# Before the first FFN: turning back by transposes, theta in the last head, the second bias behind both scales

## The chip, the cores and the metric

The kernel runs on one core of one Trainium2 chip. The metric is the device time in microseconds of one execution; several executions give a median. The profile is taken from one execution by the hardware profiler, and its times count from that execution's first instruction.

## What is computed

A block of four residual steps on x, 8 batches of 256 rows of 512 (2048 rows in all), with a context of the same shape:

```python
x = x + tanh(g_xattn[0]) * L0_xattn(ctx, ctx, layernorm(x), ssm_kernel, D, 8)
x = x + tanh(g_ffn[0])   * L0_ffn(layernorm(x), w1, b1, w2, b2)
x = x + tanh(g_xattn[1]) * L1_xattn(layernorm(x), ctx, theta, phi, g, ...)
x = x + tanh(g_ffn[1])   * L1_ffn(x, w1, g1, w2, g2, w3, g3)
```

The first step is a long convolution for each of 32 heads. The second quantises the normalised x by ONE scale for the whole tensor (max of all absolute values over 127), multiplies by int8 weights w1 (2048x512), adds b1, applies GELU, quantises by one scale again and multiplies by w2 (512x2048), with b2 added. `theta` is a product of the context alone: theta_w (128x256) by each batch's context, plus theta_b; step three uses it.

## The kernel before

The program is written by hand for each engine, with semaphores between them. The x residual stands in SBUF as 16 tiles of 128x512 (`x_res`); `order1` lists the first half of every batch's rows and then the second, so tiles n = 0 to 7 and n = 8 to 15 belong to one half each. Groups of four tiles share one computation of scales (`G` = 4, `NG` = 4).

**Heads.** TensorE computes 32 heads by 20 fp32 matmuls each (`head`, L1221 to L1237), VectorE multiplies (L1662), GpSimd and VectorE add halves into `qT`, and ScalarE repeats operands (L824, L846). Heads 20 to 27 carry the turning back of tiles 0 to 7 in spare PSUM columns (L1235), added to x by VectorE with a reversed reading of PSUM (`back_add`, L1702). ScalarE's loop over the heads (L897) also turns weights of the last FFN into ternary values (`ternary`, L885). SP's queue loads and stores those weights.

**Between the last head and the first FFN** (about 190 to 222 us):

- TensorE turns the last eight tiles back. For six tiles it first adds x itself to PSUM by a product with the identity (L1295), then multiplies by `gated`, a reversed identity times the gate (L1307, made by GpSimd at L649); ScalarE copies these six tiles out (`x1_copy`, L934), VectorE adds two (`x1_add`, L1741). Three small transposes (b1 and theta_w, L1291 and L1293) stand between. Then come the theta products (`theta`, L1309), five of them ahead of the maximum, one behind it, and two behind `rows_T(0)`.
- VectorE reduces the absolute maximum of each normalised tile (`largest`, L1717), takes statistics (L1588) and moments (L1592) of the groups 2 and 3, the maximum of all (L1754), and quantises (L1769 to L1774). In heads 28 to 30 it widens w1 (`w1_widen`, L1654).
- GpSimd computes each group's scales (`norm_scales`, L586) and adds b2 to the residual (`add_b2`, L660): tiles 0 to 3, then the scales of group 2, tile 4, the scales of group 3, tiles 5 to 7. After the quantisation it adds the last eight, and then widens the turned rows (`turned_widen`, L676).
- ScalarE normalises (L786), makes the theta results out of PSUM (`theta_out`, L946) and quantises a part (L961).
- SP's queue, in this order: the early context (2048 KB) for theta (L423), its second half behind the last head's product (L425), the first quarter of w2 (L428), `x1_save(0)` behind four bias additions, `x1_save(1)` behind eight (L434), the eight theta stores (L440), a wait until all of them have landed, the second quarter of w2 (L442), the stores of the quantised rows of groups 2 and 3 (L446), and then their turning by DMA (L451).

**The first FFN product** (`mm1`, L1339): r = 0 to 3, each 16 times 4 matmuls of 128x512. r=0 and r=1 use rows that TensorE turned itself. r=2 and r=3 use rows turned by DMA and widened by GpSimd: TensorE waits for `xq_out` to reach 4 (L1359) before r=2. ScalarE applies GELU, which for r=2 overwrites `x_res` and so waits for the saves (L985).

The lines on SP that set the order there:

```python
x1_save(0)
x1_save(1)
for b in range(NB):
    sp.wait_ge(S["th_made"], b + 2)
    sp.dma_start(th_d[b], th_made[b]).then_inc(S["k_stored"], 16)
sp.wait_ge(S["k_stored"], 16 + 16 * NB)
sp.dma_start(raw2[1], w2c[1]).then_inc(w2_in[1], 16)
```

Of the kernel before, what the change touches and what calls it, by code (L numbers as in the profile page):

```python
# [46 lines left out]
def flamingo_gated_block(nc, x_d, ctx_d, g_xattn_d, g_ffn_d, ssm_d, D_d, fw1_d, fb1_d, fw2_d, fb2_d,  # L47
# [24 lines left out]
    with ExitStack() as ctx:  # L72
# [102 lines left out]
        gated = sw2b[:, 0:P]  # L175
# [68 lines left out]
        gated_made back_tr x1_out x1_dve b2_ready xb_added st1 rs1 x1_saved amax_ready amax_all sx_ready s1_ready xqi_ready xqb_ready xq_tr xq_out  # L244
# [47 lines left out]
        dve_adds = [NT - 4, NT - 2]  # L292
        act_copies = [n for n in range(NT // 2, NT) if n not in dve_adds]

        def x1_made(eng, n):

            if n in dve_adds:
                eng.wait_ge(S["x1_dve"], 2 + NT // 2 + dve_adds.index(n) + 1)
            else:
                eng.wait_ge(S["x1_out"], act_copies.index(n) + 1)  # L300
# [45 lines left out]
        def _(sp):  # L346
# [214 lines left out]
        def _(pool):  # L561
# [76 lines left out]
            for h in range(HEADS - 3):  # L638
# [8 lines left out]
                if h == NT // 2:  # L647
                    pool.wait_ge(S["tanh_done"], 1)
                    pool.tensor_tensor(gated, bass.AP(identf[:, :].tensor, identf[:, :].offset + P - 1, [list(identf[:, :].ap[0]), [-1, P]]), tg[:, 0:1].to_broadcast([P, P]), ALU.mult).then_inc(S["gated_made"], 1)  # L649
# [131 lines left out]
        def _(act):  # L781
# [113 lines left out]

            repeat_q(0, 0)
            for h in range(HEADS - 2):  # L897
                if 1 <= h < HEADS // 2:
                    late_copy(h - 1)
                if h + 1 == HEADS // 2:  # L900
                    repeat_c(h + 2, h % 2)
                    late_copy(h)
                    act.wait_ge(S["q_out_act"], G + NT // 2)
                repeat_q(h + 1, 1 - h % 2)
                if h + 2 == HEADS // 2:
                    act.wait_ge(S["c_out"], G + NT // 2)
                if h + 1 != HEADS // 2:
                    repeat_c(h + 2, h % 2)
                if h == 1:
# [21 lines left out]
            repeat_q(HEADS - 1, 1)  # L931


            def x1_copy(n):  # L934
                act.wait_ge(S["back_tr"], n + 1 - NT // 2)
                act.activation(x_res[:, order1[n], :], ps[:, n % 8, :], ACT.Copy).then_inc(S["x1_out"], 1)
# [3 lines left out]
            act.wait_ge(S["small_in"], 96)  # L940
            act.wait_ge(S["th_tr"], 1)
            act.activation(th_w.rearrange("p d k -> p (d k)"), ps[:, 6, 0:2 * P], ACT.Copy).then_inc(S["th_made"], 1)
            act.activation(b2b[:, :], b2b[:, :], ACT.Copy, scale=tg[:, 2:3]).then_inc(S["b2_ready"], 1)
            for n in act_copies:
                x1_copy(n)
            def theta_out(b):  # L946
                act.wait_ge(S["th_tr"], b + 2)
                act.activation(th_made[b], ps[:, b % 4, :], ACT.Identity, bias=cols3[:, 0:1]).then_inc(S["th_made"], 1)

            for n in range(2 * G, 3 * G):  # L950
                normalise_x1(n)
            theta_out(0)
            theta_out(1)
            for n in range(3 * G, NT):
                normalise_x1(n)
            theta_out(2)


# [1255 lines left out]
```

## Time and profile before

| | |
|---|---|
| median of 3 runs | 635.82 us (635.71 to 637.44) |
| profiled execution, its own time | 637.47 us |
| its span, first to last instruction | 635.7 us |
| TensorE busy | 608.2 us (96%) |
| VectorE busy | 542.8 us (85%) |
| ScalarE busy | 474.3 us (75%) |
| GpSimd busy | 352.3 us (55%) |
| chain that ended last, by engine | PE 67%, DVE 13%, ACT 10%, issue 5%, DMA 2%, POOL 2% |

The profile's names: PE is TensorE (PEld its weight loads), DVE VectorE, ACT ScalarE, POOL GpSimd, SPq the instructions by which SP issues DMAs. `arena`, `turn`, `late` are large SBUF buffers that many tiles share, `ps` is PSUM. L and a number is a line of the kernel. A line of a timeline merges like instructions (x is their number), and its length is from the first's start to the last's end. Matmuls overlap, so four of them last less than four times one. "Idle before" names the instruction that ended a wait.

### The profile page before, as it was taken

The numbers are of one execution on the slowest core, as the hardware profiler recorded it, in microseconds if no ns is written. First come the engines' busy times: TensorE is split into PE (matmuls) and PEld (weight loads), VectorE is DVE, ScalarE is ACT, GpSimd is POOL, SyncE is SP. The second block draws the span as 40 slices with busy tenths as digits, with TensorE's granted clock in tenths as the row PEclk, the third lists the DMA queues.
The fourth block names the chain that finished last, engine by engine and source line by source line (L and its number), as shares of the span: only waits on it lengthen the run. The fifth ranks groups of instructions, "written<-read, shape, count | busy, mean of one in ns | idle before, by whom it ended". The sixth has DMA issues, their size and how long they took to land.

```text
span 635.7 us, 9329 instructions
## 1 busy us (share of the span) xinstructions
PE 608.2 (96%) x2775; PEld 359.6 (57%) x2804; DVE 542.8 (85%) x1066; ACT 474.3 (75%) x716; POOL 352.3 (55%) x432
## 2 busy tenths in 40 slices
PE   6899999999999999989999999999788999999996
PEld 6777777777777444444445565555333444444443
DVE  3697888889999889876779988899898999999864
ACT  3469785765764899987763487667689999999984
POOL 2589888888877454310000111114488989889861
PEclk9899999999999999999999999999999999999999
DMA  8959896799999689739359900000116666566651
GB/s 301 379 196 309 291 331 230 251 326 338 340 306 317 258 274 305 183 90 358 140 108 197 249 26 16 16 17 17 51 46 170 182 167 181 165 187 171 181 154 50
DMA packets 141989, 125.20 MB, mean 197 GB/s; under 512 B 96048, under 2 KB 104000, under 8 KB 140800
## 3 DMA queue, kind: packets, MB, share of 16 engines
q1 hardware_dynamic: 134512, 110.52, 57.4%
q10 hardware_dynamic: 7440, 14.24, 6.7%
q8 instruction: 16, 0.26, 0.2%
q14 instruction: 21, 0.17, 0.1%
HBM read 68.04 MB, written 33.64 MB: 160 GB/s over the span
## 4 chain that ended last, share of the span: by engine, by line
PE 67%; DVE 13%; ACT 10%; issue 5%; DMA 2%; POOL 2%; SPq 0%; ACTq 0%; DVEq 0%; POOLq 0%
PE ps L1226 22%; PE ps L1506 14%; PE ps L1522 8%; PE ps L1344 7%; ACT turn L1015 4%; PE ps L1433 3%; PE ps L1463 3%; PE ps L1481 2%; PE ps L1437 2%; PE ps L1235 2%; PE ps L1413 1%; PE ps L1423 1%; DMA arena<-kpad_d 1%; DVE turn L1899 1%; ACT arena L968 1%
## 5 line engine op out<-in xcount | busy, mean ns | idle before, releaser
L1226 PE MATMUL ps<-arena 128*128 128x288 f32 x640 | 160.8, 408 | 4.3 <-DMA arena<-kpad_d 2.8
L1226 PEld LDWEIGHTS ps<-arena 128*128 128x128 f32 x640 | 119.6, 190 | 36.2 <-issue 3.4
L1506 PE MATMUL ps<-arena 128*128 128x512 bf16 x510 | 113.4, 379 | 4.1 <-DVE arena L2094 4.0
L1506 PEld LDWEIGHTS ps<-arena 128*128 128x128 bf16 x512 | 49.5, 98 | 66.0 <-DVE arena L2094 3.2
L737 POOL TENSOR_TENSOR arena<-arena 128x512 f32<-128x512 f32 x64 | 80.3, 1275 | 8.9 <-DVE arena L2094 7.9
L621 POOL TENSOR_TENSOR arena<-arena 128x1024 f32<-128x1024 f32 x32 | 60.6, 1893 | 17.9 <-issue 11.3
L1522 PE MATMUL ps<-arena 128*128 128x512 bf16 x241 | 57.1, 379 | 1.9 <-ACT arena L1129 0.7
L1375 PE MATMUL ps<-arena 128*128 128x512 bf16 x251 | 55.3, 379 | 1.2 <-DVE arena L1843 0.9
L1344 PE MATMUL ps<-arena 128*128 128x512 bf16 (+1 forms) x249 | 55.4, 379 | 0.6 <-ACT arena L968 0.3
L628 POOL TENSOR_TENSOR turn<-turn 128x512 f32<-128x512 f32 x31 | 40.5, 1306 | 22.8 <-DVE turn L1678 22.8
L2094 DVE SCALAR_TENSOR_TENSOR arena<-ps,up_scale,arena 128x512 f32<-128x512 f32 x64 | 46.7, 745 | 5.8 <-ACT arena L1105 5.0
L582 POOL TENSOR_TENSOR ve<-mv,eps_ln 128x2 f32<-128x2 f32 x8 | 1.6, 196 | 87.5 <-DVE mv L1878 87.5
L968 ACT ACTIVATE arena<-ps,b,s 128x512 f32<-128x512 f32 x64 | 47.4, 793 | 3.4 <-PE ps L1344 0.3
L1105 ACT ACTIVATE arena<-ps,up_scale 128x512 f32<-128x512 f32 x64 | 42.9, 675 | 5.1 <-PE ps L1506 4.4
L1668 DVE TENSOR_TENSOR turn<-ps,arena 128x768 f32<-128x768 f32 x32 | 30.6, 955 | 18.3 <-PE ps L1235 15.5
L1344 PEld LDWEIGHTS ps<-arena 128*128 128x128 bf16 x256 | 24.9, 98 | 31.0 <-issue 1.3
L1375 PEld LDWEIGHTS ps<-arena 128*128 128x128 bf16 x256 | 24.9, 98 | 30.8 <-issue 1.0
L2101 DVE TENSOR_REDUCE q<-arena 128x1 f32<-128x1024 f32 x32 | 38.7, 1213 | 4.2 <-POOL arena L737 4.2
L1522 PEld LDWEIGHTS ps<-arena 128*128 128x128 bf16 x256 | 24.8, 98 | 30.6 <-ACT arena L1129 0.8
L731 POOL TENSOR_TENSOR arena<-turn,arena 128x1024 f32<-128x1024 f32 x16 | 37.9, 2370 | 5.5 <-ACT turn L1100 5.2
L1678 DVE TENSOR_TENSOR turn<-ps,turn 128x1024 f32<-128x1024 f32 x32 | 39.2, 1225 | 1.1
L1044 ACT ACTIVATE arena<-ps,nmx 128x512 f32<-128x512 f32 x32 | 21.8, 685 | 24.3 <-DVE nmx L1937 23.8
(232 smaller groups left out, 1281.0 us busy)
## 6 DMA issues: line engine op xcount, KB each, us to landing
arena<-in_L_ffn_w SPq DMA_DIRECT2D x48, 512.0 KB, 6.1
arena<-kpad_d ACTq DMA_DIRECT2D x16, 512.0 KB, 7.1
hq_d<-arena SPq DMA_DIRECT2D x14, 512.0 KB, 2.7
tern_d<-late SPq DMA_DIRECT2D x24, 256.0 KB, 5.4
arena<-in_ctx SPq DMA_DIRECT2D x4, 1024.0 KB, 11.4
arena<-in_L_ffn_w ACTq DMA_DIRECT2D x8, 512.0 KB, 5.8
arena<-in_ctx SPq DMA_DIRECT2D x2, 2048.0 KB, 10.6
x_d<-arena SPq DMA_DIRECT2D x4, 1024.0 KB, 5.3
```

What stands on the lines that cost most here:

```text
L621: pool.tensor_tensor(dst[:, :, 0:32].rearrange("p r (d i) -> p r d i", d=4), a, shifted, ALU.mult)
L628: po.done(pool.tensor_tensor(x[:, :, 0:16], x[:, :, 0:16], x[:, :, 16:32], ALU.add))
L737: pool.tensor_tensor(hg[:, s, sl], hh[:, s, sl], g3[:, sl], ALU.mult).then_inc(S["hg_done"], 1)
L968: act.activation(hid[:, q, f, :], ps[:, f % 4, :], ACT.Gelu, bias=b1[:, f:f + 1], scale=s1[:, f:f + 1]).then_inc(S["gelu_done"], 1)
L1105: act.activation(sil[:, c, :], ps[:, up_banks(t, c)[0], :], ACT.Silu, scale=up_scale[:, s, 0:1]).then_inc(S["sil_done"], 1)
L1226: last = pe.matmul(ps[:, 4 * s + lo, 0:NB * PAIRS], toep[:, u, (LB - 1 - lo + li) * P:(LB - lo + li) * P], kv[:, s, li, :], start=(li == 0 ...
L1344: last = pe.matmul(ps[:, f % 4, :], fw1T[:, k, f * P:(f + 1) * P], xqT[:, k, ds(L * r, L)], start=(k == 0), stop=(k == LB - 1))
L1375: return pe.matmul(ps[:, 2 * j + f // 8, :], hq[:, r % 2, f, j * P:(j + 1) * P], fw2T[:, f, :], start=(f == first), stop=(f % 8 == 7))
L1506: last = pe.matmul(ps[:, bank, :], xq4T[:, s, 4 * j + k, :], w[:, k, c * L:(c + 1) * L], start=(k == 0), stop=(k == LB - 1))
L1522: last = pe.matmul(ps[:, 7 if s == 0 else 2, :], hqT[:, s, f, :], bw3T[:, f, :], start=(f == 0), stop=(f == FT - 1))
L1678: v.tensor_tensor(half[u], y[:, :, :, 0:32], pd, ALU.add).then_inc(S["prod_done"], 1)
L2094: v.scalar_tensor_tensor(out=hh[:, s % 2, c * L:(c + 1) * L], in0=ps[:, up_banks(t, c)[1], :], scalar=up_scale[:, s, 1:2], in1=sil[:, c, : ...
```

## The change

- TensorE turns the last eight tiles by plain transposes into banks 4 to 7, with no addition in PSUM. VectorE adds tiles 8, 9, 12 and 13 with gate and reversed reading in one instruction; for tiles 10, 11, 14 and 15 ScalarE copies with gate and reversal into `turn`, and GpSimd adds.
- The small transposes of b1 and theta_w move into head 18, with their copies on VectorE.
- The context for theta is loaded in four transfers of 1024 KB, two of them issued by ScalarE in its loop at h = 29; theta 0 and 1 stand ahead of the turning, 2 to 7 directly behind it. Unread bf16 matmuls (20, 24 and 12) are put in.
- The widening of w1's first three quarters goes from VectorE to ScalarE; VectorE takes three maxima in the heads in exchange, and alternates adds, statistics and maxima behind them.
- GpSimd computes the scales of groups 2 and 3 ahead of all eight bias additions.

The diff's core:

```diff
@@ SP
-            sp.wait_ge(S["cd_ready"], HEADS)
-            sp.dma_start(ctx_early[0], ctx_rows[:, 0:NT // 2, :]).then_inc(c_in[1], 16)
             sp.wait_ge(S["prod_done"], HEADS + 2)
-            sp.dma_start(ctx_early[1], ctx_rows[:, NT // 2:NT, :]).then_inc(c_in[2], 16)
+            for part, c in ((0, 2), (1, 0)):
+                sp.dma_start(ctx_early[1][:, G * part:G * part + G, :],
+                             ctx_rows[:, NT // 2 + G * part:NT // 2 + G * part + G, :]).then_inc(c_in[c], 16)
@@ GpSimd
-            for h in range(HEADS - 3, HEADS - 1):
-                add_halves(h, h % 2)
+            add_halves(HEADS - 3, 1)
             norm_x1(1)
+            add_halves(HEADS - 2, 0)
...
+            for m, n in enumerate(pool_adds):
+                t = order1[n]
+                pool.wait_ge(S["x1_out"], m + 1)
+                pool.tensor_tensor(x_res[:, t, :], gated[:, m, :], x_res[:, t, :], ALU.add).then_inc(S["x1_pool"], 1)
...
+            norm_x1(2)
+            norm_x1(3)
             pool.wait_ge(S["b2_ready"], 1)
             pool.wait_ge(S["xn1_ready"], 2 * G)
-            add_b2(range(G))
-            norm_x1(2)
-            add_b2(range(G, G + 1))
-            norm_x1(3)
-            add_b2(range(G + 1, 2 * G))
+            add_b2(range(2 * G))
@@ ScalarE
+                if h == HEADS - 3:
+                    repeat_c(h + 2, h % 2)
+                    act.wait_ge(S["cd_ready"], HEADS)
+                    for part, c in ((0, 1), (1, 3)):
+                        act.dma_start(ctx_early[0][:, G * part:G * part + G, :],
+                                      ctx_rows[:, G * part:G * part + G, :]).then_inc(c_in[c], 16)
...
+                    if k == TC - 1:
+                        repeat_q(HEADS - 1, 1)
+                        w1_widen(1)
...
+            def gated_copy(m):
+                act.wait_ge(S["back_tr"], pool_adds[m] + 1 - NT // 2)
+                act.activation(gated[:, m, :].rearrange("p (l c) -> p l c", l=LB), turned_back(pool_adds[m]), ACT.Copy,
+                               scale=tg[:, 0:1]).then_inc(S["x1_out"], 1)
...
+            w1_widen(2)
+            theta_out(0)
             act.activation(b2b[:, :], b2b[:, :], ACT.Copy, scale=tg[:, 2:3]).then_inc(S["b2_ready"], 1)
+            theta_out(1)
+            for m in range(len(pool_adds)):
+                gated_copy(m)
+            theta_out(2)
+            theta_out(3)
+            for n in range(2 * G, NT):
                 normalise_x1(n)
@@ TensorE
+            def turn_back(n):
+                b = order1[n] // 2
+                if n >= NT // 2 + G:
+                    if n - G in dve_adds:
+                        pe.wait_ge(S["x1_dve"], 2 + NT // 2 + dve_adds.index(n - G) + 1)
+                    else:
+                        pe.wait_ge(S["x1_out"], pool_adds.index(n - G) + 1)
+                for l in range(LB):
+                    last = pe.transpose(ps[:, 4 + n % G, l * P:(l + 1) * P], qT[:, l * NB + b, P:2 * P], identf[:, :])
+                last.then_inc(S["back_tr"], 1)
+
+            pe.wait_ge(S["prod_done"], HEADS + 1)
+            theta(0)
+            theta(1)
+            pe.wait_ge(S["prod_done"], HEADS + 2)
+            pe.wait_ge(S["o_done"], HEADS + 2)
+            for n in range(NT // 2, NT):
+                turn_back(n)
+            for b in range(2, NB):
+                theta(b)
+            pe.wait_ge(S["x1_out"], len(pool_adds))
+            pe.wait_ge(S["x1_dve"], 2 + NT // 2 + len(dve_adds))
+            unread_b(20)
             pe.wait_ge(S["amax_ready"], 1)
...
+            unread_b(24)
             rows_T(0)
-            theta(G + 2)
-            theta(G + 3)
+            unread_b(12)
@@ VectorE
+                x = x_res[:, order1[n], :].rearrange("p (l c) -> p l c", l=LB)
                 v.wait_ge(S["back_tr"], n + 1 - NT // 2)
+                v.scalar_tensor_tensor(x, turned_back(n), tg[:, 0:1], x, ALU.mult, ALU.add).then_inc(S["x1_dve"], 1)
...
+            largest(3)
+            x1_add(8)
+            largest(4)
+            x1_add(9)
+            x1_stats(8)
+            x1_stats(9)
+            x1_add(12)
+            x1_stats(10)
+            x1_add(13)
+            x1_stats(11)
+            x1_moments(2)
+            for n in range(12, 16):
+                x1_stats(n)
+            x1_moments(3)
+            for n in range(5, NT):
                 largest(n)
```

SP's order behind these loads is not in the diff.

## Rows read from the trace of the kernel before

**Rows 1.** The page, busy time of the engines

```profile
PE 608.2 (96%) x2775; PEld 359.6 (57%) x2804; DVE 542.8 (85%) x1066; ACT 474.3 (75%) x716; POOL 352.3 (55%) x432
```

**Rows 2.** The chain of waits, 214 to 222 us: start, length, what

```profile
214.19 0.18 DVE am L1754
...
217.91 3.49 PE ps L1317 x8
221.45 3.40 PE ps L1344 x15
```

**Rows 3.** Timeline of VectorE, head 27 and behind the last head: start, length, instruction

```profile
176.47 0.73 DVE L1706 SCALAR_TENSOR_TENSOR arena<-ps,tg,arena 128x512 f32<-128x512 f32 x1
...
197.07 4.83 DVE L1719 TENSOR_REDUCE amax<-arena 128x1 f32<-128x512 f32 x8
201.81 2.47 DVE L1588 BATCH_NORM_STATS2 bn<-arena 128x6 f32<-128x512 f32 x4
...
204.61 1.25 DVE L1744 TENSOR_TENSOR arena<-ps,arena 128x512 f32<-128x512 f32 x2
```

**Rows 4.** Timeline of TensorE: the turning back, FFN r=3

```profile
198.09 7.31 PE L1307 MATMUL ps<-sw2b,arena 128*128 128x128 f32 x64
...
264.13 13.98 PE L1344 MATMUL ps<-arena 128*128 x62 [0.26 <-ACT arena L968]
```

**Rows 5.** Timeline of GpSimd; then VectorE's casts L1657 (min/median/max in ns)

```profile
208.74 0.20 POOL L590 TENSOR_TENSOR ve<-mv,eps_ln 128x4 f32<-128x4 f32 x1 [1.02 <-DVE mv L1592]
...
210.42 3.73 POOL L663 TENSOR_TENSOR arena<-arena,b2b 128x512 f32<-128x512 f32 x3
...
229.54 3.41 POOL L663 TENSOR_TENSOR arena<-arena,b2b 128x512 f32<-128x512 f32 x2 [15.39 <-DVE turn L1809]
...
246.25 1.90 POOL L679 TENSOR_SCALAR arena<-arena 128x2048 bf16<-128x2048 int16 x1 [3.08 <-DMA arena<-x1q_d]
...
L1657 DVE CAST arena<-arena x3: 683/684/978, 181.8 to 190.9; 128x2048 bf16<-128x2048 int16 x3
```

**Rows 6.** SP's queue, 214 to 238 us; then issues: KB each, us to landing

```profile
214.18 0.37 SPq L434 DMA_DIRECT2D x_d<-arena  x1
...
225.37 0.33 SPq L442 DMA_DIRECT2D arena<-in_L_ffn_w  x1
228.23 1.58 SPq L446 DMA_DIRECT2D x1q_d<-turn  x2
...
231.97 6.16 SPq L451 DMA_TRANSPOSE arena<-x1q_d  x1
...
arena<-in_L_ffn_w SPq DMA_DIRECT2D x1, 1024.0 KB, 4.8
...
x1q_d<-turn SPq DMA_DIRECT2D x2, 512.0 KB, 3.5
```

**Rows 7.** Stretches: length, busy of PE, PEld, DVE, ACT, POOL; PEclk, DMA share, GB/s

```profile
215.00:224.00 9.00, 8.55 (x40) 4.06 (x40) 6.59 (x13) 7.88 (x10) 0.00 (x0) 1.00 0.94 349
...
227.00:246.00 19.00, 18.89 (x88) 8.60 (x88) 18.83 (x18) 17.11 (x23) 13.63 (x9) 1.00 1.07 309
...
15.00:18.00 3.00, 0.22 (x2) 0.24 (x2) 2.96 (x9) 0.00 (x0) 2.82 (x6) 1.00 1.06 388
...
20.00:22.00 2.00, 2.00 (x11) 2.00 (x10) 0.00 (x0) 1.20 (x3) 1.11 (x2) 0.50 1.05 385
...
473.00:475.00 2.00, 0.20 (x1) 0.13 (x2) 1.97 (x5) 2.00 (x3) 2.00 (x3) 1.00 0.00 0
```

**Rows 8.** The chain of waits, 19 to 27 us: sixteen transposes, twice

```profile
19.66 3.24 PE ps L1197 x16
...
24.36 1.75 PE ps L1197 x16
```

**Rows 9.** ScalarE's timeline, 188 to 190 us; then its casts L1057 (ns)

```profile
188.45 1.15 ACT L889 ACTIVATE late<-arena,inv_s 128x1024 int16<-128x1024 f32 x1 [4.14 <-DMA arena<-in_L_ffn_w]
...
L1057 ACT ACTIVATE arena<-arena x12: 1893/1926/1934, 367.2 to 440.5; 128x2048 bf16<-128x2048 int16 x12
```

More of the change, by code:

```diff
@@ L291, in flamingo_gated_block @@
         FIRST_TURN = 20
-        dve_adds = [NT - 4, NT - 2]
-        act_copies = [n for n in range(NT // 2, NT) if n not in dve_adds]
+        dve_adds = [n for n in range(NT // 2, NT) if n % G < 2]
+        pool_adds = [n for n in range(NT // 2, NT) if n % G >= 2]
+        gated = turn[:, 0:4 * L].rearrange("p (m l) -> p m l", m=4)
         def x1_made(eng, n):
@@ L299, in x1_made, with turned_back @@
             else:
[L300 removed]
+                eng.wait_ge(S["x1_pool"], pool_adds.index(n) + 1)
+        def turned_back(n):
+            y = ps[:, 4 + n % G, :].rearrange("p (l c) -> p l c", l=LB)
+            return bass.AP(y.tensor, y.offset + P - 1, [list(y.ap[0]), [P, LB], [-1, P]])
         def xn1_of(t):
@@ L894, in normalise_x1, with w1_widen @@
                 normalise_tile(xn1_of(order1[n]), order1[n], n, S["xn1_ready"])
+            def w1_widen(c):
+                w = fw1T[:, :, c * L:(c + 1) * L]
+                act.wait_ge(S["w1_in"], 16 * c + 16)
+                act.activation(w, w.bitcast(I16), ACT.Copy).then_inc(S["w1_ready"], 1)
             repeat_q(0, 0)
@@ L906, in _ @@
                     act.wait_ge(S["c_out"], G + NT // 2)
-                if h + 1 != HEADS // 2:
+                if h + 1 != HEADS // 2 and h != HEADS - 3:
                     repeat_c(h + 2, h % 2)
+                if h == HEADS - 3:
+                    w1_widen(0)
                 if h == 1:
@@ L973, in _ @@
             quant_x(0)
-            for b in range(3, G + 2):
-                theta_out(b)
+            theta_out(6)
+            theta_out(7)
             quant_x(1)
-            for b in range(G + 2, NB):
-                theta_out(b)
             act.activation(warm[:, :], eps_ln[:, 0:1], ACT.Gelu)
@@ L1218, in _, with small_T @@
             pe.wait_ge(S["c_out_dve"], G)
+            def small_T(s):
+                pe.wait_ge(S["small_in"], 96)
+                pe.transpose(ps[:, 4 * s, NB * PAIRS:NB * PAIRS + FT], b1n, identf[0:FT, 0:FT])
+                for d in range(2):
+                    last = pe.transpose(ps[:, 4 * s + 1 + d, NB * PAIRS:NB * PAIRS + P], th_raw[:, d, :], identf[:, :])
+                return last
             def head(h, s, late, between=None):
@@ L1236, in head @@
                                             late[l], identf[:, :])
+                if h == HEADS // 2 + 2:
+                    last = small_T(s)
                 last.then_inc(S["y_ready"], 1)
@@ L1276, in _ @@
                     pe.wait_ge(S["x1_dve"], b + 1)
+                if b == 0:
+                    pe.wait_ge(S["b1_out"], 1)
+                    pe.wait_ge(S["th_made"], 1)
                 head(h, h % 2, [qT[:, l * NB + b, 0:P] for l in range(LB)])
@@ L1283, in _ @@
                 head(HEADS - 4 + u, u % 2, None)
[L1286 to L1308 removed]
             def theta(b):
[L1310 to L1313 removed]
+                if b % 2 == 0:
+                    pe.wait_ge(c_in[(1, 3, 2, 0)[b // 2]], 32)
                 if b >= G:
@@ L1319, in theta, with unread_b @@
                 last.then_inc(S["th_tr"], 1)
-            for b in range(G + 1):
-                theta(b)
+            def turn_back(n):
[16 more added lines that the diff above has]
+            for b in range(2, NB):
+                theta(b)
+            pe.wait_ge(S["x1_out"], len(pool_adds))
+            pe.wait_ge(S["x1_dve"], 2 + NT // 2 + len(dve_adds))
+            def unread_b(times):
+                for n in range(times):
+                    pe.matmul(ps[:, 6, n % 4 * P:(n % 4 + 1) * P], identb[:, :], identb[:, :], start=True, stop=True)
+            unread_b(20)
             pe.wait_ge(S["amax_ready"], 1)
             pe.transpose(ps[:, 7, 0:P], am1[:, 0:1].to_broadcast([P, P]), identf[:, :]).then_inc(S["amax_all"], 1)
-            theta(G + 1)
-            pe.wait_ge(S["x1_out"], len(act_copies))
-            pe.wait_ge(S["x1_dve"], 2 + NT // 2 + len(dve_adds))
             def rows_T(g):
```

92 lines of the change are left out of this document (23 added, 69 removed).

## The prediction

> **What bounds the kernel now.** I read the page first. TensorE is busy 96% of the span [rows 1], so what counts is when TensorE gets work. Then I read the chain of waits from the last head to the FFN. It leaves TensorE at 197.07, when VectorE has made the last head's addition, goes through GpSimd's bias adds and scales, ScalarE's normalising and VectorE's maxima, and reaches the overall maximum at 214.19; two theta products (eight matmuls, 3.49 us) then stand between the quantised rows and the first FFN matmul at 221.45 [rows 2]. From there TensorE runs back to back. Last I read the queues beside the chain. The part r=2 of the first FFN product needs rows that SP stores and turns and GpSimd widens; that widening ends at 246.25+1.90 = 248.15 [rows 5]. The part r=3 begins at 264.13, and its 62 recorded matmuls fill 13.98 us, so 64 of r=2 fill 14.0 before it and begin at 250.1 [rows 4]. This side path has a slack of 1.95 us, and every gain ahead of it eats slack.
>
> **The gains.** *TensorE.* The turning costs 7.31 us as 32 products (64 records) [rows 4], besides the identity products ahead of it. Sixteen transposes took 1.75 [rows 8], so the 32 of the last eight tiles cost 3.5. VectorE sets the pace instead. From 197.07 until it has the moments of all groups it does two maxima of 0.60, two groups of statistics and moments of 2.80 each (201.81 to 204.61), and four adds. Such an add (reversed PSUM, gate, residual) lasts 0.73 with its overlap, a plain one takes 0.63; I take 0.66 [rows 3]. The sum is 1.2+5.6+2.7 = 9.5 us; before, it was there at 208.7 [rows 5].
>
> *Head 18* gets three transposes, 0.33 us [rows 8], and two small copies on VectorE, mostly in its slack: 0.4 on TensorE's path, between 0.3 and 0.8. The moments are then ready at 197.07+0.4+9.5 = 207.0, 1.7 earlier. *ScalarE* takes three casts of 1.93 and two DMA issues; it sat idle for 4.14 us before its last weight piece alone [rows 9], and again behind the last head until GpSimd had the second group's scales. I cost them at nothing; without that cover its four gated copies come late, GpSimd's adds behind them. *GpSimd's* four adds, 1.24 each (3.73 for three [rows 5]), end about 204.6, when group 2's moments are there; they have 1 us of room.
>
> *Maxima and theta.* Eleven maxima remain behind 207.0, so the overall one comes at 213.6 against 214.19 [rows 2]: the stage itself gains 0.6 us. The two theta products leave the path: up to 2.9 more. The fillers on TensorE, 56 small bf16 matmuls, lie in its waits and cost nothing unless its clock is low.
>
> **The moved bias, the term that decides.** Before, five of the first eight bias adds lay ahead of or between the scales and three at 210.42 [rows 5], and SP issued the second save at 214.18 [rows 6]. Now all eight stand behind the last scales: 207.0 + 1.7 (the scale instructions, 208.74 to 210.42) = 208.7, then 8 x 1.24 = 9.9, so 218.6. On SP this save (1024 KB) stands ahead of the eight theta stores (256 KB each), and SP waits until they all have landed before it loads the second quarter of w2 (225.37) and stores the rows for r=2 (228.23) [rows 6]. That theta is made earlier doesn't help: its stores are queued behind the save.
>
> *The port.* A VectorE cast of 0.68 took 0.98 while GpSimd was in the middle of an addition, and two additions from 229.54, beside a VectorE quantisation, took 3.41 instead of 2.5 [rows 5]. VectorE's quantising and casts now fall among the eight adds: I take 1.0 us for GpSimd, between 0 and 1.6, so the save goes at 219.6. The Trainium skill, "SBUF — State Buffer", section "Who interferes with whom", says that the shared port pair is held for a whole instruction and the other side fully blocks; the trace agrees in both directions. By that rule the three VectorE pieces could each wait for one whole add, up to 2.5 us ahead of the FFN where one cast shows 0.3, which would take most of the gain at the first FFN matmul; but that gain is waited away below.
>
> *SP.* From that save to SP's release it was 11.2 us. The 3.15 MB moved at 349 GB/s from 215 to 224, while the same engines moved 388 where they were full, from 15 to 18 [rows 7]; with all stores ready this saves 0.6 or more, of which I take 0.6: 10.6. SP is free at 230.2, 4.9 later. The w2 load lands 4.8 after issue [rows 6], and the first 512 KB of rows behind it on the same queue take 1.4 more (at 388), so the first turning goes 6.4 after SP is free, at 236.6 against 231.97: +4.7. (If that store landed in its usual 3.5 [rows 6] in spite of the load ahead, it would be +2.2 or so: the low end.) The turning, the save and the second turning behind it keep their length, since the DMA engines were full (share 1.07) in those 19 us [rows 7]. The widening ends at 252.9, and TensorE can start r=2 at 252.9 instead of 250.1: **+2.8 us**.
>
> **The clock.** TensorE, 1 to 2 us early, then idles from 248 or 249 to 252.9, some 4 us. In this trace the granted clock fell to 0.50, the 1.2 GHz level, after TensorE had been busy 0.22 of the 3 us from 15 to 18; it did not fall around 473 to 475, with 0.20 busy of 2 us [rows 7]. Sixteen transposes in the low stretch took 3.24 instead of 1.75 [rows 8]: 1.5 us more. A gap longer than both makes a fall likely, and r=2 is on the path: **+1.5 us**, between 0 and 2.5. The idle time before 213.6 may do the same, but ahead of a wait.
>
> **Sum.** 2.8+1.5 = 4.3 us on the span of 635.7. The profiled execution took 637.47, 1.65 over the median of the runs, 635.82; I put the shift on the median: **640.1 us**. A measurement of this kernel can tell about 0.3%, 1.9 us, from no change.
>
> **Rivals.**
> - *Late, clock held* (0.22): the same queue, no fall: 638.6.
> - *Absorbed* (0.15): SP's chain is late by only 2 to 3 us and the slack of 1.95 takes most: 636.3. For it: before, the rows were stored 2.5 us behind the release's load, time that a late release can use up. Against it: the w2 load is then directly ahead of them.
> - *Faster* (0.09), the other side: r=2 doesn't wait. This decides if the second widening ends by 248 or so, that is, if the late save doesn't reach it. Then the theta products count: 0.6+2.9 (head 18 is in the 0.6 already), less about 1.1 for the port: 2.4 us, 633.4. Against it stands the save, which can't go before 218.
> - *Worse* (0.06): ScalarE's two 1024 KB loads share the DMA engines with the last weight load, for which ScalarE already waits 4.14 us [rows 9]; beyond 1 us of room, each microsecond moves the gated copies and the bias adds too. 1.5 us more: 641.6.
> - The forecast itself has 0.48.
>
> The upper bounds (2.5 for the clock, 1.6 for the port, the worse case) reach 643.0; leaving out the faster case and part of the absorbed one, the low end is 636.2. Faster by over 0.3%: 0.09; within: 0.15; slower: 0.76.
>
> **What would show it.** Right: the last of GpSimd's first eight bias adds near 219 and SP's second save behind it; the w2 load near 230; the first turning near 236.6; TensorE idle 3 us or more before r=2 until GpSimd's widening, then a stretch of clock below 1; the maximum near 213.6; the first FFN matmul 1 to 2 us earlier. Wrong: no gap before r=2; SP's second save before 217; a first FFN matmul later than 221.45, which would make the port or a cold TensorE the cause and not the queue.

## The result, and the profile after

The changed kernel takes 642.21 us (median of 5; 640.91 to 643.85), the kernel before 637.44 in the same measurement (635.71 to 637.53): ratio **1.0083**, 95% interval 1.0068 to 1.0097. That is a small loss, but a clear one. The profiled executions have spans of 640.4 and 635.7 us: +4.7. TensorE's share falls from 96% to 95% [rows 1]. Below, "the heads end" stands for the end of the last head's matmuls on TensorE, and "third round" for r=2 of the first FFN product, the first part that needs the rows turned by DMA.

The chain of waits of the changed kernel from the last head on (start, length, what) is now the queue, not the maximum:

```profile
194.13 1.15 ACT late L893
...
202.32 3.73 POOL arena L664 x3
...
210.63 10.45 POOL arena L669 x8
221.10 0.37 SPq L439
...
227.71 2.99 DMA th_d<-sw2b
230.72 0.33 SPq L447
...
231.10 7.37 DMA x1q_d<-turn
238.48 6.01 SPq L456
...
245.16 6.93 DMA arena<-x1q_d
...
252.16 1.91 POOL arena L683
...
254.52 1.68 PE ps L1371 x7
```

Read it from the end. TensorE's third FFN round waits for GpSimd's widening (L683), this for the turning's transfer, this for SP, SP for the landing of the theta stores, these for the save (L439), and the save for the eighth bias add (L669). Against [rows 6]: save 221.10 (the second one was issued at 214.18), w2 load 230.72 (225.37), first turning 238.48 (231.97).

TensorE's timeline, changed kernel (start, length, then what; in brackets the idle time before it and what ended it):

```profile
124.31 0.23 PE L1241 MATMUL ps<-identf,arena 16*128 16x16 f32 x1
...
130.09 5.09 PE L1251 MATMUL ps<-arena 128*128 128x288 f32 x20 [0.33 <-DVE arena L1750]
135.01 0.60 PE L1260 MATMUL ps<-identf,arena 128*128 128x128 f32 x4
...
220.00 1.03 PE L1363 MATMUL ps<-identb,turn 128*128 128x128 bf16 x8 [2.61 <-DVE turn L1815]
...
223.46 3.62 PE L1371 MATMUL ps<-arena 128*128 128x512 bf16 x16
...
254.52 7.66 PE L1371 MATMUL ps<-arena 128*128 x34 [2.38 <-POOL arena L683]
```

The small transposes stand at 124.31, TensorE then waits 0.33 us for their copies, and head 20's transposes come at 135.01; in the trace of before they came at 133.77: +1.24. The heads end at 194.06 (192.07 before); 0.6 of the rest is a wait of 0.59 us in head 22 for a load of the heads' convolution matrix (`kpad_d`). The first FFN matmul is at 223.46, 2.0 later than in [rows 2]. The third round is at 254.52. In the kernel before it began at about 249.9: TensorE had 112 matmuls from 225.58 on, which take 24.34 us in the changed kernel and in the traces below. So it is 4.6 later.

What takes up the gain ahead of the first FFN matmul is in VectorE's timeline of the changed kernel, the quantisation and the two casts of the first rows (GpSimd's adds below them):

```profile
216.80 1.74 DVE L1812 TENSOR_SCALAR turn<-arena,isx 128x1024 int16<-128x1024 f32 x1
218.57 1.37 DVE L1815 CAST turn<-turn 128x1024 bf16<-128x1024 int16 x1
219.86 1.49 DVE L1817 CAST turn<-turn 128x1024 bf16<-128x1024 int16 x1
...
210.59 10.49 POOL L669 TENSOR_TENSOR arena<-arena,b2b 128x512 f32<-128x512 f32 x8
```

The same three in the kernel before, where GpSimd was idle beside them:

```profile
215.49 0.75 DVE L1769 TENSOR_SCALAR turn<-arena,isx 128x1024 int16<-128x1024 f32 x1
216.28 0.43 DVE L1772 CAST turn<-turn 128x1024 bf16<-128x1024 int16 x1
216.67 0.43 DVE L1774 CAST turn<-turn 128x1024 bf16<-128x1024 int16 x1
```

Each piece is about 1 us longer, 3.0 in all; one add is 1.24. The maximum itself came 0.7 earlier behind the heads than before (215.50 and 214.19, so 21.4 and 22.1 behind them), near the 0.6 forecast.

**A measure.** In eleven of the fourteen executions profiled, TensorE's granted clock dips near 20 us, for a longer or a shorter time, in three it doesn't. This moves all that follows by up to 3 us (one group of 16 transposes at 19 to 21 us takes 1.9 to 3.5), so the traces are compared by distances from the end of the heads. In us, from each trace:

| kernel | heads end | first FFN matmul | third round | TensorE's wait ahead of it | end of span | median |
|---|---|---|---|---|---|---|
| before | 192.07 | +29.4 | +57.9, no gap | 0 | +443.6 | 637.4 |
| changed | 194.06 | +29.4 | +60.5 | 2.38 | +446.3 | 642.2 |
| changed again | 193.50 | +29.6 | +60.1 | 2.02 | +447.7 | 640.9 |
| save late | 191.69 | +29.5 | +59.5 | 1.53 | +445.4 | 641.9 |
| bias behind casts, save late | 193.33 | +26.8 | +58.8 | 3.55 | +446.5 | 641.2 |
| port only | 195.16 | +26.2 | +63.1 | 8.42 | +451.2 | 645.9 |
| save in the hole | 191.53 | +26.2 | +55.8 | 1.16 (not for rows) | +441.7 | 637.2 |
| small ones behind heads | 192.20 | +28.9 | +57.4, no gap | 0 | +443.1 | 636.5 |
| before, bias last | 192.14 | +33.0 | +61.7, no gap | 0 | +449.1 | 641.5 |
| no fillers | 192.17 | +29.3 | +60.9, no gap | 0 | +446.8 | 640.5 |
| bias early | 195.00 | +28.1 | +58.0 | 1.19 (not for rows) | +443.9 | 638.9 |

"Changed again" is the same kernel measured once more, at the end of the section on experiments, where the other kernels are explained; the median is that of all executions of each. Where TensorE had no gap, the start of the third round is worked out with the 24.34 us. Some traces lack one of the first 16 FFN matmul records (that of before too), so the column of the first FFN matmul can be 0.2 too high there.

The 4.7 us are thus: heads 2.0, third round behind them 2.6 (2.4 of it TensorE's wait), rest 0.1. The first FFN matmul is as far behind the heads as before, within 0.2.

### The profile page after: what moved, and what is told of

The parts are those of the page before. It is cut to its first block, busy times and chain, and to the rows that moved or that the text cites. A ratio compares the mean times of both kernels' runs of the same rounds, so it can differ in the third digit from the quotient of the medians.

```text
span 640.4 us, 9387 instructions
## 1 busy us (share of the span) xinstructions
PE 608.0 (95%) x2816; PEld 358.9 (56%) x2816; DVE 545.1 (85%) x1066; ACT 478.6 (75%) x716; POOL 356.2 (56%) x435
## 3 DMA queue, kind: packets, MB, share of 16 engines
q1 hardware_dynamic: 133488, 108.43, 55.8%
## 4 chain that ended last, share of the span: by engine, by line
PE 55%; DVE 11%; ACT 9%; DMA 8%; SPq 7%; issue 5%; POOL 4%; ACTq 0%; DVEq 0%; POOLq 0%
PE ps L1533 14%; PE ps L1251 13%; PE ps L1549 8%; SPq L406 4%; PE ps L1460 3%; PE ps L1490 3%; PE ps L1402 3%; DMA arena<-in_L_ffn_w 2%; PE ps L1371 2%; ACT turn L1032 2%; PE ps L1508 2%; PE ps L1464 2%; POOL arena L669 2%; PE ps L1440 1%; PE ps L1450 1%
## 5 line engine op out<-in xcount | busy, mean ns | idle before, releaser
L626 POOL TENSOR_TENSOR arena<-arena 128x1024 f32<-128x1024 f32 x32 | 60.6, 1892 | 20.0 <-issue 11.4
L1371 PE MATMUL ps<-arena 128*128 128x512 bf16 (+1 forms) x256 | 56.1, 379 | 2.6 <-POOL arena L683 2.4
```

What stands on the lines that cost most here:

```text
L626: pool.tensor_tensor(dst[:, :, 0:32].rearrange("p r (d i) -> p r d i", d=4), a, shifted, ALU.mult)
L1371: last = pe.matmul(ps[:, f % 4, :], fw1T[:, k, f * P:(f + 1) * P], xqT[:, k, ds(L * r, L)], start=(k == 0), stop=(k == LB - 1))
```

## Experiments

Each was timed beside the kernel before (medians 637.0 to 637.4), in three measurements. The changed kernel stood in the last one only, with the kernels called port only, save in the hole and small ones behind the heads; the others are compared with it through their ratios to the kernel before.

### The moved bias alone, in the kernel before

```diff
-            add_b2(range(G))
             norm_x1(2)
-            add_b2(range(G, G + 1))
             norm_x1(3)
-            add_b2(range(G + 1, 2 * G))
+            add_b2(range(2 * G))
```

> The kernel before with one edit: GpSimd's eight bias adds all behind both scales, as in the changed kernel; nothing else. Bias theory (this part alone carries the loss, the other parts about cancel): the adds run from 210.4 to about 220.5 beside VectorE's quantisation and casts, which take 4.6 us instead of 1.6; the first FFN matmul comes up to 3 us later than 221.45; the second save goes at 220.3 instead of 214.2, the w2 load near 230, and the third FFN round at 254 to 254.5: 640.5 to 642. Rival, the loss is in the other parts (small transposes in a head, fp32 transposes back, ScalarE's longer list): 637 to 638, no more than the port's share.

Measured: 641.49, ratio 1.0066 (1.0045 to 1.0087). The bias theory's time holds, its way only in part. VectorE's timeline of this kernel, then GpSimd's:

```profile
215.63 1.56 DVE L1767 TENSOR_SCALAR turn<-arena,isx 128x1024 int16<-128x1024 f32 x1
217.23 1.37 DVE L1770 CAST turn<-turn 128x1024 bf16<-128x1024 int16 x1
218.52 1.49 DVE L1772 CAST turn<-turn 128x1024 bf16<-128x1024 int16 x1
```

```profile
210.47 10.66 POOL L663 TENSOR_TENSOR arena<-arena,b2b 128x512 f32<-128x512 f32 x8
```

The first FFN matmul comes at 225.17, 3.7 later, more than the 3.0 expected: the two theta products ahead of it take 4.44 us here, not 3.49 [rows 2], with the granted clock at 0.69 from 220 to 224. The queue is late as well, by about as much as in the changed kernel: GpSimd has the widened rows 60.6 behind the heads (60.0 in the changed kernel, 56.1 before). But TensorE is then so late that they are ready 1.1 us ahead of it. Here it is the long casts (the "port", from the prediction's word for what VectorE and GpSimd share) that take the time; in the changed kernel, which brings TensorE there sooner, the queue takes part of it. (The profiled execution is 1.5 above the median; 1.0 of that is two waits for DMAs at 519 and 524 us.) One edit to the kernel before costs 4.1 us of its 637.4, as much as the whole change within the noise, so the other parts of the change about cancel.

### Queue alone: the second save behind the row stores

```diff
             x1_save(0)
-            x1_save(1)
...
             x1q_store(3)
+            x1_save(1)
             w2_store(0)
```

> The changed kernel with one move on SP's queue: the save of x tiles 4 to 7 is issued behind the two row stores instead of ahead of the theta stores. All arithmetic as in the changed kernel. Queue theory (the save waited for GpSimd's last bias add until 221.1 and held the theta stores, the w2 load at 230.7 and the first turning at 238.5): the w2 load goes near 225, the first turning at 234 to 235, the third FFN round starts when TensorE is free (252.1 instead of 254.5), and the kernel takes about 638.0, 1.004 of the kernel before. Rival, start alone (the 2 us by which the first FFN matmul is late and VectorE's long casts set everything behind): unchanged, 640.4. Rival, clock: a TensorE that no longer waits 2.4 us changes nothing else, since its clock was 1.00 there; if more than 2.4 us is won, the clock had a share.

Measured: 641.92, ratio 1.0069 (1.0044 to 1.0093), spread over 638.93 to 642.51. The queue theory's 638.0 was missed. The profiled execution took 638.93, but its heads ended 2.4 us earlier than the changed kernel's; from their end it is 0.9 us shorter, not 2.4. SP's timeline, then TensorE's:

```profile
223.86 0.33 SPq L446 DMA_DIRECT2D arena<-in_L_ffn_w  x1
228.00 1.58 SPq L450 DMA_DIRECT2D x1q_d<-turn  x2
...
232.85 7.24 SPq L455 DMA_TRANSPOSE arena<-x1q_d  x1
```

```profile
251.22 5.14 PE L1371 MATMUL ps<-arena 128*128 x22 [1.53 <-POOL arena L683]
```

The w2 load is free as expected, but the turning now starts 9.0 us behind it, and takes 7.2. Of the 9.0, SP waits 3.8 for the quantised rows, which come as far behind the heads as before (the row stores are 36.3 behind them, before 36.2). The turning took 6.16 before [rows 6]; the held-back save (1024 KB) now stands between the row stores and it. A megabyte taken off the queue's head came back behind it.

### Port and queue: bias adds of tiles 4 to 7 behind the casts, save late

```diff
-            add_b2(range(2 * G))
+            add_b2(range(G))
+            pool.wait_ge(S["xqb_ready"], 2)
+            add_b2(range(G, 2 * G))
```

and the save moved as above.

> The changed kernel with the save of tiles 4 to 7 behind the row stores, and GpSimd's bias adds of tiles 4 to 7 behind VectorE's two casts of the first group, so that GpSimd is idle while VectorE does its quantisation and casts. Port theory (1.74, 1.37 and 1.49 us instead of 0.75, 0.43 and 0.43 because GpSimd's adds ran beside them): the three are back at their short times, the first FFN matmul starts 2 to 3 us earlier than 223.46, at 220.5 to 221.5, the adds of tiles 4 to 7 end near 224 where nobody waits, and with the queue free the time is 635.5 to 636.5, level with the kernel before. Rival, queue alone: 638.0 as with the save moved by itself. Rival, late adds hold the save and through it the w2 quantisation or the later saves: over 638.

Measured: 641.19, ratio 1.0059 (1.0041 to 1.0078). Half right: the first FFN matmul is at 26.8 behind the heads, as the port theory said, and the time is not: TensorE waits 3.55 us. TensorE's timeline, then three of the stretches (TensorE's granted clock is the third figure from the end, then DMA share and GB/s):

```profile
252.17 1.48 PE L1373 MATMUL ps<-arena 128*128 x6 [3.55 <-POOL arena L685]
```

```profile
232.00:236.00 4.00, 4.00 (x21) 1.81 (x19) 4.00 (x2) 3.51 (x6) 4.00 (x5) 1.00 1.07 397
...
248.00:252.00 4.00, 0.62 (x3) 0.10 (x1) 3.93 (x4) 1.35 (x2) 1.90 (x1) 1.00 1.12 373
252.00:256.00 4.00, 3.61 (x11) 1.56 (x13) 2.33 (x2) 1.55 (x2) 0.00 (x0) 0.69 1.02 317
```

The first turning, issued at 233.42, took 8.71 us, with the DMA engines full (share 1.07 from 232 to 236): the order of the bytes decides. And behind this wait the clock fell, which the changed kernel's own profile did not show: from the third round to the end it is 387.6 us here and 385.9 there, 1.7 more.

### Port alone: adds behind the casts, save in its old place

The diff is that of GpSimd above, without the save's.

> The changed kernel with GpSimd's bias adds of tiles 4 to 7 behind VectorE's casts and nothing else: the save of those tiles stays ahead of the theta stores. It sets the two theories against each other. Both true: first FFN matmul 26.8 behind the heads, 2.6 better than in the changed kernel, but the save only at 224 to 224.5, theta stores until 231, w2 load at 234, first turning at 242, third FFN round at 257 to 258 with TensorE waiting 6 us and its clock at 0.50 behind that: 644 to 646. If only the port matters: 639 to 640. If only the queue: over 644 and the first FFN matmul at 29.4 behind the heads.

Measured: 645.92, ratio 1.0134 (1.0107 to 1.016). This run sets the two theories apart, and both hold: first FFN matmul at +26.2, and a wait of 8.42 us that eats far more than the 3 us won. (6 us were expected; the time is in the range expected.) SP's timeline, TensorE's, and a stretch (TensorE's clock third from the end):

```profile
234.43 0.33 SPq L447 DMA_DIRECT2D arena<-in_L_ffn_w  x1
...
243.50 4.71 SPq L456 DMA_TRANSPOSE arena<-x1q_d  x1
```

```profile
258.27 2.74 PE L1373 MATMUL ps<-arena 128*128 x6 [8.42 <-POOL arena L685]
```

```profile
256.00:260.00 4.00, 1.73 (x5) 0.71 (x6) 3.93 (x5) 0.00 (x0) 1.81 (x1) 0.50 1.04 314
```

### The save in the queue's hole

```diff
             x1_save(0)
-            x1_save(1)
             for b in range(NB):
...
+            x1_save(1)
             sp.wait_ge(S["k_stored"], 16 + 16 * NB)
             sp.dma_start(raw2[1], w2c[1])...
```

with GpSimd's adds behind the casts.

> The changed kernel with two edits: GpSimd's bias adds of tiles 4 to 7 behind VectorE's two casts, and the save of these tiles between SP's theta stores and its wait for them, in the stretch (223 to 226) where the queue waits and the DMA engines are three quarters idle. Measured from the end of the heads. Port and queue theory together: quantisation and casts short, first FFN matmul 26.8 behind the heads (29.4 in the changed kernel), row stores landing in 3.5 to 4.5 us instead of 6.1 since the save is no longer between them and the turning, third FFN round at 56 to 57 (58.8 with the save behind the row stores), span 441.8 to 442.8 behind the heads against 443.6 of the kernel before, and with the heads 1.24 later by the small transposes: 636.0 to 637.5, level with the kernel before. Rival, transfers: the same bytes ahead of the second turning, third round again near 58.8, 639 to 640.

Measured: 637.22 against 637.41 for the kernel before and 640.90 for the changed kernel beside it; ratio 1.0011 (0.9996 to 1.0027): no difference from before that can be told. VectorE's pieces are short again; SP's timeline, then TensorE's:

```profile
214.06 0.75 DVE L1814 TENSOR_SCALAR turn<-arena,isx 128x1024 int16<-128x1024 f32 x1
214.84 0.43 DVE L1817 CAST turn<-turn 128x1024 bf16<-128x1024 int16 x1
```

```profile
221.17 0.37 SPq L439 DMA_DIRECT2D x_d<-arena  x1
224.01 0.33 SPq L447 DMA_DIRECT2D arena<-in_L_ffn_w  x1
224.94 1.58 SPq L451 DMA_DIRECT2D x1q_d<-turn  x2
...
231.50 4.84 SPq L456 DMA_TRANSPOSE arena<-x1q_d  x1
```

```profile
247.37 14.14 PE L1373 MATMUL ps<-arena 128*128 x62 [1.16 <-ACT arena L989]
```

The save rides behind the theta stores while SP waits for their landing; the w2 load is issued 3 us behind it. The rows are turned from 40.0 behind the heads on (44.4 in the changed kernel), and TensorE's wait is now for ScalarE's GELU and no longer for them. The row stores landed 6.5 us after issue, not in the 3.5 to 4.5 expected, but they went out earlier. The adds that were held back now run beside a later cast (0.69 us in the changed kernel, 1.74 here), for which nobody waits. One save moved and one wait added give back the loss, with the same transfers and adds as in the changed kernel. Against "port and queue" above, the place of the save is all that differs: 641.19 there. What the save in the hole gives without the held-back adds was not run.

### And the small transposes behind the heads

In addition: the three transposes after the last head, 60 unread matmuls in the gap that follows, all thetas behind the tiles turned back, ScalarE's gated copies ahead of its thetas.

```diff
-                if h == HEADS // 2 + 2:
-                    last = small_T(s)
...
             pe.wait_ge(S["prod_done"], HEADS + 1)
-            theta(0)
-            theta(1)
+            small_T()
+            for n in range(60):
+                pe.matmul(ps[:, 1, n % 4 * P:(n % 4 + 1) * P], identb[:, :], identb[:, :], start=True, stop=True)
```

> As the kernel with the save between the theta stores and their wait, and the small transposes out of head 18: they stand behind the last head, followed by 60 unread 128x128 bf16 matmuls in TensorE's gap, the tiles turned back, and then all eight thetas; ScalarE does its four gated copies ahead of the thetas; VectorE copies th_w and b1 behind its last halving. Head theory: the heads end 1.24 earlier (192.1 with the clock dip at 20 us), the copies give 0.4 to 0.6 back, 635.3 to 636.8, 0.3 to 0.8 below its companion. Rival, theta in a row behind the transposes is too late (ends 3.5 later, near the maximum at 214): the amax transpose waits behind it, up to 1 us back, no gain. Rival, clock: the gap or the fillers leave the transposes back at half clock, 2 us more.

Measured: 636.52, ratio 0.9988 (0.9975 to 1.0001), 0.7 below the kernel with the save in the hole, as expected; the lowest of all, and against the kernel before no difference that this measurement proves. Head 20's transposes are back at 133.90. A part of the gain went elsewhere, as ScalarE's timeline shows:

```profile
208.60 0.69 ACT L962 ACTIVATE arena<-ps,cols 128x512 f32<-128x512 f32 x1 [1.03 <-PE ps L1318]
209.19 5.74 ACT L792 ACTIVATE arena<-arena,shift,rstd 128x512 f32<-128x512 f32 x8
```

The group's scales were there at 206.3, but four theta outputs stand ahead of the normalising, the last until 209.2; so the first FFN matmul is at +28.9 instead of +26.2. Putting them behind it is the next thing to try; it wasn't run.

### The bias of tiles 0 to 3 early

```diff
             add_halves(HEADS - 2, 0)
+            pool.wait_ge(S["b2_ready"], 1)
+            pool.wait_ge(S["xn1_ready"], G)
+            add_b2(range(G))
             pool.wait_ge(S["o_done"], HEADS + 2)
```

> The changed kernel with the bias adds of tiles 0 to 3 (normalised since the heads) done by GpSimd between its last halving and the last widening, in its idle time at 195 to 199, and the bias scaled by ScalarE in its own wait for the last weight. The adds of tiles 4 to 7 stay behind both scales. All times against the end of the heads (194.1 in the changed kernel, 192.1 in the kernel before), because that end moves by 1.6 us with TensorE's clock at 20 to 22 us. Port theory: the adds end 5 us earlier, before VectorE's quantisation, whose three instructions fall from 1.74, 1.37, 1.49 to 0.75, 0.43, 0.43; the first FFN matmul comes 26.8 us behind the heads instead of 29.4 (26.83 was seen with the adds held back). Queue theory: the second save at 21.5 behind the heads instead of 27, theta stores from then, w2 load near 31.5, third FFN round at 57 to 58 behind the heads instead of 60.5. Time 637.0 to 639.5. Rival, port moved: the four early adds run beside VectorE's last halving and first additions and hold these by up to 2 us, 640. Rival, moved bias without weight: 641 to 642 as the changed kernel.

Measured: 638.89, ratio 1.0037 (1.0012 to 1.0061): both the port theory and its rival. The casts are short again (0.75, 0.43, 0.43), but VectorE's last halving now meets the early adds:

```profile
198.85 1.51 DVE L1762 TENSOR_TENSOR turn<-turn 128x512 f32<-128x512 f32 x1
200.39 1.38 DVE L1764 TENSOR_TENSOR arena<-turn 128x256 f32<-128x256 f32 x1
```

The same two took 0.69 and 0.42 in the changed kernel; its operations that read PSUM, right ahead of them, kept their lengths beside the same adds. The first FFN matmul is at +28.1, not at the 26.8 expected. With the second w2 load behind the row stores as well:

> As the kernel with four early bias adds, and the second w2 load (1024 KB) issued behind SP's two row stores instead of ahead of them. Transfer theory (from 228 on the DMA share is 1.0 and more; with the save held back the row stores landed 6.1 us after issue behind that load and the first turning took 8.7 us, and TensorE waited 3.6 us for it although the queue was free): the row stores land in 3 to 3.5 us, the turning starts 2 us earlier, and the third FFN round starts when TensorE is free, 55.5 us behind the heads: 635.5 to 636.5, level with or below the kernel before. Rival: VectorE then waits for the w2 chunk (maxima at 40 us behind the heads), 637 to 638. Rival, total bytes: the same megabytes stand ahead of the last turning in any order, no gain over the kernel with four early adds.

Measured: 640.68, ratio 1.0055 (1.0034 to 1.0075). Neither theory: between the row stores and the first turning there is now one 1024 KB load more, and this turning takes 9.9 us instead of 4.9. Its heads were followed by a wait of 3.41 us, behind which the 32 transposes took 6.64 us (3.9 to 4.4 in the changed kernel and those with the save moved, 5.35 with the bias early), so its trace says little of the rest.

### Two orders that cost five microseconds

Small transposes behind the heads, but theta still ahead of the tiles turned back:

> The changed kernel with the three small transposes and the two VectorE copies taken out of head 18 and put between the last head and theta. Head theory (they cost the heads 1.2 us by themselves, and the 0.7 us at head 22 is their consequence): the last addition of the heads ends 1.2 to 2.0 earlier than 198.97, and the first FFN matmul starts as much earlier less some 0.4 for the copies, at 221.9 to 222.7. What the end makes of it: if the third FFN round hangs on GpSimd's bias adds and these on ScalarE's last weight (194.13, by a transfer that no head sets), the time stays within 0.5 of 640.4; if that weight was itself late by the heads, the time falls by 1.2 to 1.6, to about 639. Rival, noise between executions (0.7 to 1.7 us among runs of one kernel): the heads end at 198.9 as in the changed kernel.

Context loads on SP again:

> The changed kernel with ScalarE's two 1024 KB context loads issued by SP again, behind its last stores, as in the kernel before. Theory that these loads held up the last weight (its load was issued 3.1 us later than before but landed 5.7 us later): the last weight comes 2 to 2.6 us earlier, near 191.5, GpSimd's four adds start up to 1.3 us earlier than 202.3 (TensorE's transposes bound them then), the bias adds end near 219.8 and the time falls by 1.0 to 1.3, to 639.1 to 639.4. Rival, the loads were free: last weight at 194 and 640.4. Rival, theta's loads become late on SP: theta ends later than 218 and the row stores with it, 641 or more.

Measured: 645.18, ratio 1.0125 (1.0102 to 1.0148), and 646.57, 1.0139 (1.0115 to 1.0162). Both expectations missed what TensorE's timelines show, the first line of the one kernel, the second of the other:

```profile
199.06 5.26 PE L1316 MATMUL ps<-arena 128*128 128x512 f32 x8 [4.98 <-DVE b L1775]
```

```profile
198.08 6.34 PE L1322 MATMUL ps<-arena 128*128 128x512 f32 x8 [4.77 <-DMA arena<-in_ctx]
```

Two thetas stand ahead of the transposes in TensorE's order, and whatever they wait for (copies that I had put behind VectorE's last halving; a load) holds the tiles. That ScalarE issues these loads early is worth 5 us to the changed kernel. The second run also shows what ScalarE's loads did to the last weight: without them it is there 3.0 us ahead of the heads' end (190.27), in the changed kernel 0.1 behind it (194.13). It was delayed, and it didn't matter: when the changed kernel was measured again it came 1.2 ahead of the heads' end (192.26), and the eighth add still ended 26.9 behind the heads, in the first 27.0.

### The fillers, and the changed kernel again

```diff
-            unread_b(20)
-            unread_b(24)
-            unread_b(12)
```

> The changed kernel without the 56 unread 128x128 matmuls around the maximum's transpose and the first rows; nothing is computed from them. Clock theory (they keep TensorE's granted clock up while it has no other work from 211 to 223): without them the stretch from 216 to 224 is at 0.50, the sixteen row transposes and the first FFN matmuls run at half speed, and the first FFN round loses 1 to 2 us, 643 to 644; the third round's late chain may absorb it, since TensorE waited 2.4 us there: then 642.2. Rival, they do nothing (the clock fell to 0.58 in 220 to 224 in spite of them, and the first FFN matmuls ran at 1.00): no change.

Measured: 640.50, ratio 1.0053 (1.0032 to 1.0075). TensorE's first FFN matmuls:

```profile
221.45 6.57 PE L1370 MATMUL ps<-arena 128*128 128x512 bf16 x16 [0.99 <-DVE arena L1820]
```

6.57 us instead of 3.62, at a clock of 0.50 from 220 to 224 and 0.57 from 224 to 228. With the fillers it is 0.58 and 1.00: they don't keep the clock from falling at 220, but it is back when the FFN starts, and without them it isn't. That is worth 3 us at this place, and the third round's late rows take the 3 us back. Nothing is left at the end, as the expectation had allowed for.

> The changed kernel itself, unedited, beside the others. Both theories: ratio to the kernel before near 1.008 as measured, 641.5 to 643; three long casts; the first FFN matmul 29.4 behind the heads, the third FFN round 60.5 behind them. If the wait of 0.6 us for the Toeplitz load in head 22 is an accident of one execution, it need not show again, and the heads then end at 193.3; if the change causes it, it does.

Measured: 640.90, ratio 1.0049 (1.0029 to 1.0068); with the first measurement, the change costs 0.5 to 0.8%. The three long casts (1.88, 1.37, 1.49) and the late third round show again. Two stretches show what the first profile had not:

```profile
252.00:256.00 4.00, 2.37 (x6) 0.93 (x7) 3.93 (x5) 0.84 (x2) 1.16 (x1) 0.71 1.05 306
256.00:260.00 4.00, 3.78 (x16) 1.72 (x16) 2.11 (x2) 2.94 (x5) 0.00 (x0) 0.86 1.07 330
```

Behind a wait of 2.02 us the clock fell; behind 2.38 us in the first it had not. From the third round to the end it is 387.6 us here and 385.9 in the first: 1.7 more.

## Why the prediction was right, and where it was not

640.1 was forecast, +4.3 on the span; +4.7 came. (The time measured, 642.21, is further off because the kernel before also came out higher this time, 637.44 and not 635.82.) The largest part, 2.6 us, came by the mechanism that had most of the chance, the late rows. The nearness of the sum is in part luck, as the items show.

- **The queue: right, to the microsecond.** Put against the end of the heads, the forecast save was 27.1 behind it (219.6 against 192.47) and 27.0 was measured; from the save to the first turning 17.0 and 17.4; from there to the widened rows 16.3 and 15.6. Inside the second stretch two errors cancel: SP was free 9.6 behind the save, not 10.6, and the first turning came 7.8 behind that, not 6.4, because the row store behind the w2 load took 7.4. The start of r=2 before was read 0.2 too late (250.1 for 249.9; the row shows 0.26 idle ahead of r=3), so the slack was 1.8 and not 1.95.
- **Head 18: mis-sized.** "0.4 on TensorE's path, between 0.3 and 0.8" was 1.24: the transposes take 0.43, TensorE waits 0.33 more for VectorE's copies, and the next head starts behind both. Without them head 20's transposes came at 134.05 and 133.90, near the 133.77 of before. Of the rest, 0.7 lies in head 22, with the wait for the convolution matrix. The spacing of heads 21 and 22 is 0.2 to 1.2 us longer than elsewhere in seven traces of the changed kernel and those built from it (one without the small transposes among them), and not in five; what causes it stays open.
- **The port: right on GpSimd, wrong on VectorE.** GpSimd's eight adds took 10.49 us, 0.6 more than 9.9 (I took 1.0). On VectorE I let about 0.3 stand for each piece, from one cast; the three cost 3.0. The Trainium skill, "SBUF — State Buffer", section "Who interferes with whom", says that the other side blocks for a whole instruction. By that rule three adds of 1.24 would be up to 3.7 us, an estimate, not the 2.5 that the prediction has; 3.0 lies between. So the first FFN matmul was 2.0 late (the heads' 2.0) and not 1 to 2 early, which the text had named as a sign against it. That sign was half right: the port has its part in the loss, but the queue's is there beside it, as the runs with one of the two alone show. Without the adds beside the casts and with the save in the hole, the first FFN matmul came 4.8 behind the maximum's transpose, before 7.0 behind: 2.3 won, where the forecast had up to 2.9 for theta.
- **The clock: mis-sized by that.** TensorE came late itself and waited 2.4 us instead of 4. In the profiled execution the clock held: 0 instead of 1.5. When the kernel was measured again it fell behind a shorter wait (2.02), and 1.7 us went, as with the wait of 3.55. The price was right, then; whether it is paid differs between executions.
- The two errors nearly cancel, and that is luck: 1.6 more in the heads, 1.5 less in the clock, 0.3 elsewhere (0.2 of it the reading of r=2). The upper bounds of the prediction add up to 643.2, not 643.0.
- **Costed at nothing:** ScalarE's loads did delay the last weight, by 2 to 3 us against the heads; the case *Worse* had that right, but the delay did not reach the bias adds.
- *Faster* asked that the save not reach the rows. With the save in the hole and the adds held back that is so (the third round then waits for GELU), and behind the heads this kernel is 1.9 us shorter than before. The result is level with before all the same, not 2.4 us faster: head 18 takes 1.24 of it.

## What to carry to other kernels

Work put off on one engine is paid by all that stands behind its consumer in an in-order queue: look for the hole in that queue (here SP's wait for a landing) and put the late item there, and not merely further back, where its bytes delay the next one. A row of GpSimd instructions beside a chain of short VectorE ones that touch SBUF alone costs each of these about a microsecond here, so it pays to keep GpSimd off the stretch that TensorE waits for; beside other VectorE work the same adds cost nothing that counted. A gain at one bound shows only when the next bound has been moved too: the port alone left the kernel 8.5 us slower than before, port and queue together brought it level.

## What the runs showed of the hardware

- Beside GpSimd adds of 1.24 us, VectorE's quantisation of 0.75 us took 1.56 to 1.88 and casts of 0.43 took 1.37 and 1.49, in seven traces alike; a cast of 0.69 took 1.74, in four traces. Fp32 additions in SBUF of 0.69 and 0.42 took 1.51 and 1.38, where operations that read PSUM (0.96, 1.22, 1.23) kept their length.
- A row store (512 KB) right behind a 1024 KB load on the same queue landed 7.4 us after issue, against 3.5 [rows 6], where it was issued 2.9 us behind the load.
- The granted clock behind an idle TensorE isn't the same in each execution: it held after waits of 2.38 and 2.57 us (the latter with the context loads on SP) and fell after waits of 2.02 and 2.27 (the latter with the rows first). In two traces in which it fell, the rest of the kernel took 1.7 us more.
